# The second level of a blockwise triangular inverse on 32x32 tiles instead of zero-padded 64x64 ones

## The reference, cut to what matters

```python
S = S * jnp.exp(g_t)[..., None, None]
kv = jnp.einsum('bhk,bhkv->bhv', k_t, S)
delta = (v_t - kv) * b_t[..., None]
S = S + jnp.einsum('bhk,bhv->bhkv', k_t, delta)
o = jnp.einsum('bhk,bhkv->bhv', q_t, S)
```

## Time and profile before

| | |
|---|---|
| device time, median of 3 runs | 2404.33 us (2402.9 to 2404.34) |
| profiled execution: span from first to last instruction | 2401.2 us (3.1 us below the median of the runs; no other time of this execution is given) |
| granted PE clock, mean | 0.981 of full speed |
| PE busy | 2317.9 us, 97% of the span |
| DVE busy | 2111.3 us, 88% |
| ACT busy | 1425.7 us, 59% |
| POOL busy | 1066.8 us, 44% |
| 16 DMA queues, mean | 50 GB/s |

### The profile page before, as it was taken

One profiled execution on the slowest core, in us unless ns is written; L12 is line 12 of the kernel. 1 busy time (PEld: TensorE's weight loads), 2 busy tenths in 40 slices (PEclk: granted clock), 3 DMA queues, 4 the chain that ended last, 5 costly groups with the idle time before them and its releaser, 6 DMA issues. The chain is left out here.

```text
span 2401.2 us, 55407 instructions
## 1 busy us (share of the span) xinstructions
PE 2317.9 (97%) x19896; PEld 1640.4 (68%) x19896; DVE 2111.3 (88%) x4579; ACT 1425.7 (59%) x3891; POOL 1066.8 (44%) x1543
## 2 busy tenths in 40 slices
PE   5899999999999999999999999999999999888998
PEld 3677767777777777776767777777777776773554
DVE  8999999998989999999999999999999989648776
ACT  5566666656565666666666666665555555333665
POOL 3634354444434354545343544444343535214564
PEclk8999999999999999999999999999999999788999
DMA  5211122222212112222221222221111011002000
GB/s 139 64 45 47 39 53 52 55 53 55 53 50 48 47 45 63 61 64 62 57 61 41 60 58 64 62 64 38 38 33 34 19 36 22 17 19 119 23 23 27
DMA packets 289390, 120.76 MB, mean 50 GB/s; under 512 B 211510, under 2 KB 267094, under 8 KB 288604
## 3 DMA queue, kind: packets, MB, share of 16 engines
q1 hardware_dynamic: 289116, 117.21, 18.5%
HBM read 85.42 MB, written 31.74 MB: 49 GB/s over the span
## 5 line engine op out<-in xcount | busy, mean ns | idle before, releaser
L1450 DVE SCALAR_TENSOR_TENSOR d_y<-bank,d_cw,d_y 128x508 f32<-128x508 f32 (+2 forms) x576 | 421.9, 733 | 6.3 <-ACT d_y L1205 0.8
L794 POOL TENSOR_SCALAR d_ms<-d_sso 128x4 f32<-128x4 f32 x64 | 14.5, 226 | 573.6 <-ACT d_junk L1343 573.6
L778 POOL TENSOR_TENSOR d_V<-d_tok,d_kinv 128x640 f32<-128x640 f32 (+1 forms) x128 | 130.3, 1038 | 303.8 <-issue 301.9
L1628 DVE SCALAR_TENSOR_TENSOR x<-bank,x 128x512 f32<-128x512 f32 x256 | 172.3, 677 | 51.3 <-PE bank L1018 51.3
L1205 ACT ACTIVATE d_y<-bank,d_cw 128x512 f32<-128x512 f32 x192 | 131.2, 684 | 88.6 <-PE bank L859 86.1
L1328 ACT ACTIVATE d_thg<-bank 128x384 f32<-128x384 f32 x128 | 62.2, 486 | 199.3 <-PE bank L973 196.9
L1614 DVE SCALAR_TENSOR_TENSOR d_on<-d_O,d_rn,d_gate 128x192 f32<-128x192 f32 x256 | 154.8, 663 | 0.0
L824 POOL TENSOR_SCALAR d_K<-d_tok,d_Em 128x96 f32<-128x96 f32 x256 | 151.3, 607 | 0.0
L1254 ACT ACTIVATE d_tok<-bank 128x384 f32<-128x384 f32 x256 | 125.5, 490 | 36.1 <-PE bank L875 32.1
L1212 ACT ACTIVATE d_th<-d_y 128x512 f32<-128x512 f32 x192 | 121.6, 634 | 41.3 <-DVE d_y L1456 34.8
L1471 DVE SCALAR_TENSOR_TENSOR d_yv<-d_th,d_y 128x512 f32<-128x512 f32 x128 | 98.2, 767 | 52.1 <-ACT d_th L1212 44.5
(11 more groups left out here) (341 smaller groups left out, 7115.4 us busy)
## 6 DMA issues: line engine op xcount, KB each, us to landing
lt_blocks<-d_LT SPq DMA_DIRECT2D x64, 256.0 KB, 2.4
d_fw<-turned_gate_w SPq DMA_DIRECT2D x32, 256.0 KB, 3.0
d_XT<-x_blocks SPq DMA_DIRECT2D x128, 64.0 KB, 2.3
d_X<-x_blocks SPq DMA_DIRECT2D x128, 64.0 KB, 2.3
d_fw<-turned_val_w SPq DMA_DIRECT2D x32, 256.0 KB, 3.0
d_fw<-turned_out_w SPq DMA_DIRECT2D x32, 256.0 KB, 2.8
d_st<-in_L_attn_Wg_dram SPq DMA_DIRECT2D x16, 384.0 KB, 4.2
ternary<-d_ft SPq DMA_DIRECT2D x48, 128.0 KB, 2.1
```

Of the source, the lines that this page charges most:

```text
L778: last = nc.gpsimd.tensor_tensor(V[q][:, :, lo:hi], tok[q][:, :, at:at + hi - lo], over(kinv[:, :], 2, hi - lo), ALU.mult)
L1450: nc.vector.scalar_tensor_tensor(out=yy[:, :, tap:], in0=pp[:, :, 0:P - tap], scalar=cw[:, ds(st.kp, 1), t, 3 - tap], in1=yy[:, :, tap:], ...
L1628: nc.vector.scalar_tensor_tensor(out=xs, in0=bank[(4, 7, 6, 5)[i]][:, :], scalar=1.0 / (SO * SW), in1=xs, op0=ALU.mult, op1=ALU.add).then_ ...
```

## The change

The level from 32 to 64 works on the 32x32 blocks that carry values. Partitions are cut in four quarters; `up` is the upper, `low` the lower quarter of a half. Nothing else in the order of any engine's list is moved. `Y32` becomes 32 columns wide and loses its memset, so all waits on `const_ready` count one less. The mask is no longer applied, since only the lower quarters are copied; the copy is two ACT instructions of 32 partitions, with one semaphore signal on the second.

```diff
-        "Y32": sb("Y32", [P, B, HB]),
+        "Y32": sb("Y32", [P, B, HB // 2]),
...
-            nc.gpsimd.memset(Y32[:, :, :], 0.0).then_inc(s["const_ready"], 1)
...
-            pool.wait_ge(s["const_ready"], 7)
+            pool.wait_ge(s["const_ready"], 6)
...
+            quarters = tuple((slice(h, h + HB // 2), slice(h + HB // 2, h + HB)) for h in (0, HB))
...
             def y_32(st):
                 hold(pe, s["X_ready"], 7 * st.n + 4)
                 for i in range(B):
-                    for h, hf in enumerate(half):
-                        last = nc.tensor.matmul(lev[hf, 3 * P + i * 32:3 * P + (i + 1) * 32], LT[st.p][hf, i, hf], X[hf, h, i, 0:32], start=True, stop=True)
+                    for h, (up, low) in enumerate(quarters):
+                        last = nc.tensor.matmul(lev[low, 3 * P + i * 32:3 * P + (i + 1) * 32], LT[st.p][up, i, low], X[up, h, i, 0:32], start=True, stop=True)
                 last.then_inc(s["yps_done"], 1)
 
             def x_32(st):
                 hold(pe, s["Y_ready"], 2 * st.n + 1)
                 for i in range(B):
-                    nc.tensor.matmul(lev[0:HB, i * 32:(i + 1) * 32], XT[0:HB, i, 0:HB], Y32[0:HB, i, 0:32], start=True, stop=True)
-                    for h, hf in enumerate(half):
-                        last = nc.tensor.matmul(lev[hf, P + i * 32:P + (i + 1) * 32], Y32[hf, i, :], XT[hf, i, h * HB + 32:(h + 1) * HB],
-                                                start=True, stop=True)
+                    first = quarters[0][1]
+                    nc.tensor.matmul(lev[first, i * 32:(i + 1) * 32], XT[first, i, first], Y32[first, i, :], start=True, stop=True)
+                    for up, low in quarters:
+                        last = nc.tensor.matmul(lev[up, P + i * 32:P + (i + 1) * 32], Y32[low, i, :], XT[low, i, low], start=True, stop=True)
                 last.then_inc(s["xps_done"], 1)
...
                 def copy_y32():
                     past(a, "yps_done", 3 * n + 2)
-                    nc.scalar.activation(Y32[:, :, 0:32], lev[:, 3 * P:4 * P].rearrange("p (b e) -> p b e", b=B), ACT.Copy,
-                                         scale=cst[:, C_MK + 2:C_MK + 3]).then_inc(s["Y_ready"], 1)
+                    for low in (slice(HB // 2, HB), slice(HB + HB // 2, P)):
+                        last = nc.scalar.activation(Y32[low, :, :], lev[low, 3 * P:4 * P].rearrange("p (b e) -> p b e", b=B), ACT.Copy)
+                    last.then_inc(s["Y_ready"], 1)
```

More of the change, by code:

```diff
@@ L238, in _ @@
             nc.gpsimd.memset(XT[:, :, :], 0.0).then_inc(s["const_ready"], 1)
-            nc.gpsimd.memset(Y32[:, :, :], 0.0).then_inc(s["const_ready"], 1)
             nc.gpsimd.memset(YJ[:, :, :], 0.0).then_inc(s["const_ready"], 1)
             nc.gpsimd.memset(nround[:, :], -ROUND).then_inc(s["const_ready"], 1)
-            pool.wait_ge(s["const_ready"], 7)
+            pool.wait_ge(s["const_ready"], 6)
             for e, tile in enumerate((X[HB:P, 0, :, :], wo[0][1][HB:P, 1, :], wo[1][1][HB:P, 1, :])):
                 nc.gpsimd.memset(tile, 0.0).then_inc(s["const_ready"], 1)
-                pool.wait_ge(s["const_ready"], 8 + e)
+                pool.wait_ge(s["const_ready"], 7 + e)
             pool.wait_ge(cst_in, 32)
@@ L839, in _ @@
             nc.gpsimd.memset(ones[:, :], 1.0).then_inc(s["const_ready"], 1)
-            hold(pool, s["const_ready"], 16)
+            hold(pool, s["const_ready"], 15)
             all_steps(step)
@@ L844, in _ @@
         def _(pe):
-            pe.wait_ge(s["const_ready"], 15)
+            pe.wait_ge(s["const_ready"], 14)
             def projection(st, j, part, parts):
@@ L1089, in step @@
                                                  start=(e == 0), stop=(e == KC - 1))
-                        pe.wait_ge(s["const_ready"], 17)
+                        pe.wait_ge(s["const_ready"], 16)
                         for e in range(KC):
@@ L1425, in step @@
                         what()
-            a.wait_ge(s["const_ready"], 15)
+            a.wait_ge(s["const_ready"], 14)
             all_steps(step)
@@ L1714, in step @@
                 if n == 1:
-                    v.wait_ge(s["const_ready"], 18)
+                    v.wait_ge(s["const_ready"], 17)
                 for go, what in ((T_, keyscale), (T_, masked), (R_ and n > 0, y16), (P_, lambda: conv(st, 0, 1)), (P_, lambda: conv(st, 0, 2)), (R_, products), (P_, lambda: conv(st, 0, 3)),
@@ L1727, in _ @@
             nc.vector.memset(S[:, :, :], 0.0).then_inc(s["S_ready"], B)
-            v.wait_ge(s["const_ready"], 14)
+            v.wait_ge(s["const_ready"], 13)
             v.wait_ge(s["block_in"], 48)
```

## The result

The changed kernel takes 2363.21 us (median of 4 runs, 2356.22 to 2369.75) against 2403.61 for the kernel before beside it: ratio 0.9839, 95% interval 0.9818 to 0.9861. Five more runs on another occasion gave 2365.13 (2361.96 to 2367.74; 0.9845, 0.983 to 0.9861). The forecast was 2376 with 2366 to 2397: the direction is right, but 38 to 40 us were saved where 28 were forecast. The profiled run has a span of 2354.4 us at a mean granted clock of 0.985.

The account below looks back on a forecast made before the run. It took PE's list to set three steps of a head (c = 1, 2, 3) and DVE's the fourth (c = 0). 16 x (0.63 + 0.50 + 0.63 + 0) = 28.2 us off gave 2376 us, range 2366 to 2397.

Parts of the forecast that it names:

- Two regimes, c = 1, 2, 3 set by PE: Per head, PE's list sets three steps and DVE's sets c = 0; cheaper matmuls pay only in the three.
- `y_32` 0.21 us: PE's `y_32` keeps two parallel tiles; 8 slots lose 26.5 ns each, 0.21 us per step.
- The slot of 32 ns from the stationary width: On PE, an f32 record with 32 stationary columns takes 32 ns instead of 58, by a line through wider ones.
- I take turns, the middle one: In `x_32`, tiles (1, 1) and (1, 0) share an input quarter and alternate: 16 slots lose 26.5 ns, 0.42 us.
- the case named beside it, 8 slots: In `x_32`, the tiles run beside each other and 8 slots of 32 ns remain: 0.68 us gained.
- The copy at no cost: ACT's copy in two pieces takes 0.45 us instead of 0.37, yet `x_32` finds it done: cost nothing.
- the slower rival: PE drains between 32x32 tiles in one input quarter, 0.8 us per step against 0.63 gained: 2412 us; chance 0.06.
- the width rival: Width does not set the slot; an f32 record takes at least 50 ns: 10 us gained, 2395 us; chance 0.13.
- The caps: Later PE waits limit gains: c = 2 to 0.50 us; with parallel tiles, c = 1 about 0.83, c = 3 0.67.
- the rival of DVE and POOL: DVE and POOL eat a part: one more collision per head (0.8 us) costs 13 us, about 2389 us; chance 0.14.
- c = 0 gains nothing: In the c = 0 step DVE's list sets the pace: 0 gained, PE's wait of 0.67 us grows to 1.3.
- would move up with PE, into DVE's way: In c = 2, POOL's work on the values would collide with DVE's rounding of weights: gain 0.50, between 0.44 and 0.63.

Follow-up runs that it names:

- e5: Kernel before, with the new form (both matmul groups and the copy) only in the 48 steps with c > 0: 2369.2 us, ratio 0.9877.
- e7: Kernel before, with POOL's product of the values left out in the c = 0 steps from the second head on: 2389.36 us, ratio 0.9955.
- e6: Changed kernel, with `x_32`'s first matmul on the same array tile as its second, both for the first half: 2370.32 us, ratio 0.9872.
- e3: Kernel before, with only ACT's copy changed to two pieces of 32 partitions without mask: 2401.46 us, ratio 0.999.
- e9: Kernel before, plus a filler of unread f16 matmuls (36 records) in step n = 62: 2390.64 us, ratio 0.9967.
- e8: Changed kernel, plus a filler of unread f16 matmuls (36 records) in step n = 62: 2357.2 us, ratio 0.9822.

## Why the prediction was wrong in size

Its steps in order:

- *Two regimes, c = 1, 2, 3 set by PE:* right. e5 took 27.6 us from these steps, each ending at a wait that had been named. The busy times that it was read from don't show it, though: in c = 0 PE is busy 29.28 us and DVE 29.09, not the other way round. What carries it is PE's wait of 0.67 us there, and e7.
- *`y_32` 0.21 us:* right, 0.214. *The slot of 32 ns from the stationary width:* the number is right, 0.373 us for 8 slots and the change of shape, and 0.619 in e6 for 16. That the width alone sets it is not shown for 32 columns, since the number of rows went to 32 with it.
- *`x_32`, "I take turns, the middle one", 0.42 us:* wrong. It gained 0.668; the case named beside it, 8 slots, said 0.68. What `L944` and `L946` do today on one tile says nothing of two tiles that share only their input partitions. The Trainium skill ("TensorEngine Tiling (Array Packing)", Key Properties) states that different tiles can execute load and matmul in parallel, without a condition on shared partitions; e6 against the changed kernel (0.619 and 0.378 us) agrees. I had weighed the first sentence of that list and passed over the second. In the first 62 steps this is worth 2.8 us, and up to 5.5 with the c = 1 steps described under e6.
- *The copy at no cost:* right (e3), though at 0.55 us and not 0.45: the second piece starts 0.28 us after the first, signal or none.
- *No added drain, the slower rival:* refuted. The records go from tile to tile in 12 ns on average. The 25 ns from start to start that the prediction quotes beside the width rival is undercut across tiles; on one tile no slot here is below 32 ns.
- *The caps.* c = 2 at 0.50: measured 0.50. c = 1 at 0.83 for side-by-side tiles: the median step gained 0.83, the mean 0.66, because two of 16 steps lost 0.04 and 0.08 us (five in e6) and two more gained only 0.30 and 0.44. This is the rival of DVE and POOL in small: DVE's L1615 is held up 0.9 us and PE waits for it through ACT. The prediction saw that chain for c = 3 alone, and its "0.8 us of play" isn't what the numbers beside it give (31.9 less 30.4 is 1.5). c = 3 was capped at 0.52, not 0.67: the chain `high`, `tap0`, `copy_yj`, `x_join` is as worked out, but DVE's L1614 did move. It ended 8.58 us into the step before (1330.65 - 1322.07) and 8.73 after (1310.89 - 1302.16), its four instructions taking 3.08 us instead of 2.96.
- *"c = 0 gains nothing":* wrong, the dearest step, and the very sign that the prediction had named against itself ("A c = 0 step that gets shorter"): 0.47 x 16 = 7.5 us. DVE does set this step, but the length of its list isn't a constant. It holds a hold-up of 0.67 us on average (0.82 less 0.15), whose end hangs on POOL, whose start hangs on PE. The fear that POOL "would move up with PE, into DVE's way" was raised for c = 2; in c = 0 the same motion took POOL out of DVE's way. L1534 with 1.13 us beside 0.15 in the other steps stood in the trace of before, and asking of every DVE instruction that is longer than its like would have found it.

The sum, by way of e6, which is the forecast's case of taking turns: 28.2 forecast; c = 0 adds 0.43 x 16 = 6.9 there; the cap of c = 3 takes 0.12 x 16 = 1.9; the c = 1 steps that gained nothing take 4.3 (a mean of 0.37 against a median of 0.64); the step from e6 to the changed kernel adds 5.5. That gives 34.4, against 2.14 x 16 = 34.2 by the mean lengths. The first 62 steps hold 32.9 of it. The medians show 38 to 40. The remaining 5 to 7 us lie behind. At nearly the same clock (e9 and e8) that part still differs by 3.2 us, 0.9 of it in step n = 62; the others go with its clock, on which the prediction had no term.

e6 is the case that was forecast, and its ratio of 0.9872 is 30.7 us, close to 28.2. That is partly chance: 0.43 x 16 = 6.9 us of it came from c = 0.

What stays open: why the granted clock behind the steps differs by a few hundredths between runs of the same kernel (0.93 and 0.90 in the two profiles), and whether the change shifts it; and what decides in a c = 1 step on which DVE instruction the hold-up falls.

## What to carry to other kernels

When one engine gets faster, don't take the other engines' lists as fixed: search them first for instructions longer than their like, and ask whose start sets that length and whether it moves along. Array tiles count by their own position: two that share only input partitions ran side by side here, so count the slots of the busiest single tile of a packed level. And when the time of two runs differs by more than the steps do, compare the granted clock stretch by stretch before crediting the change.

## What the runs showed of the hardware

- An f32 matmul record with 32 stationary columns and 32 rows takes 32 ns on its tile (0.52 us for 16 in e6), after 58 for 64 by 64 and 110 for 128 by 128; three tiles together reached one record per 12 ns.
- A DVE addition of 8 elements (0.146 us alone) lasted up to 1.22 us beside a POOL product of 640 elements, and ended some 20 ns after it.
- A hold-up of 0.9 us falls on one DVE instruction or on its neighbour, and the length of the step goes with it: 0.83 us gained or 0.08 lost for the same change.
- A filler of matmuls that nobody reads raised the granted clock of the last part from 0.89 to 0.94, and the kernel before became 0.3% faster (0.9967, 0.9951 to 0.9984) with 36 matmuls added.
- Two ACT copies of 32 partitions follow each other at 0.28 us, whether the first signals or not.
